# In each chunk of the projections, VectorE takes the row maxima of the fourth turn before the statistics of the next rows, and the variances directly follow the statistics

## The reference

```
def attention(x, Wq, Wk, Wv, Wo, bo):
    q, k, v = (split_heads(x @ W) for W in (Wq, Wk, Wv))
    scores = einsum('bhqd,bhkd->bhqk', q, k) * 16 ** -0.5
    scores = where(causal, scores, -inf)
    out = softmax(scores) @ v
    return merge_heads(out) @ Wo + bo

x = x + attention(layernorm(x), ...)
x = x + int8_matmul(layernorm(x), rhs)
```

## Time and profile before

| | us |
|---|---|
| runs of the kernel before | 1672.59, 1675.17, 1675.41 |
| their median | 1675.17 |
| the profiled execution, device time | 1670.0 |
| its span, first to last instruction | 1668.2 |
| TensorE busy | 1562.9 (94%) |
| VectorE busy | 1522.0 (91%) |
| ScalarE busy | 1362.6 (82%) |
| GpSimd busy | 290.9 (17%) |
| mean granted clock of TensorE | 0.981 |

### The profile page before, as it was taken

One profiled execution on the slowest core, in us unless ns is written; L12 is line 12 of the kernel. 1 busy time (PEld: TensorE's weight loads), 2 busy tenths in 40 slices (PEclk: granted clock), 3 DMA queues, 4 the chain that ended last, 5 costly groups with the idle time before them and its releaser, 6 DMA issues.

```text
span 1668.2 us, 40684 instructions
## 1 busy us (share of the span) xinstructions
PE 1562.9 (94%) x16715; PEld 623.8 (37%) x16715; DVE 1522.0 (91%) x1839; ACT 1362.6 (82%) x2659; POOL 290.9 (17%) x397
## 2 busy tenths in 40 slices
PE   4799989999999999999999999999999999999965
PEld 2444433333333333333333333333333333344433
DVE  5589889999999999999999999999999999578876
ACT  3355559999999999999999999999999999877651
POOL 5343401211111111111121111120202020100120
PEclk9899999999999999999999999999999999999986
DMA  2454320101121212111111212121212142034532
GB/s 82 141 161 144 124 65 17 51 18 51 43 63 43 63 52 55 57 50 60 47 60 47 60 47 59 47 61 52 62 51 63 48 119 78 15 116 134 154 118 70
DMA packets 105613, 118.79 MB, mean 71 GB/s; under 512 B 20688, under 2 KB 87508, under 8 KB 105428
## 3 DMA queue, kind: packets, MB, share of 16 engines
q1 hardware_dynamic: 105428, 116.19, 23.4%
HBM read 66.81 MB, written 48.76 MB: 69 GB/s over the span
## 4 chain that ended last, share of the span: by engine, by line
DVE 54%; PE 27%; DMA 1%; ACT 1%; issue 1%; SPq 1%; POOL 0%; ACTq 0%; DVEq 0%
DVE pmax L355 46%; PE psum L1155 12%; PE psum L1136 6%; DVE pblk L355 4%; PE psum L263 3%; PE psum L1196 3%; PE psum L277 2%; PE psum L282 2%; DMA f_rs<-inverse_sums 1%; DVE V L1438 1%; ACT prob L1326 1%; DVE V L1457 1%; DVE V L1445 1%; PE psum L1220 1%; DVE f_amax L1463 1%
## 5 line engine op out<-in xcount | busy, mean ns | idle before, releaser
L1326 ACT ACTIVATE prob<-psum 128x512 f32<-128x512 f32 (+1 forms) x2304 | 1180.9, 574 | 136.4 <-PE psum L1136 113.0
L355 DVE TENSOR_REDUCE pmax<-psum 128x2 f32<-128x1024 f32 (+1 forms) x960 | 1100.9, 1216 | 12.7 <-PE psum L282 6.6
L1155 PE MATMUL psum<-prob,V 128*32 128x256 f32 x8704 | 675.7, 391 | 0.0
L1136 PE MATMUL psum<-Q,K 50*128 50x512 f16 (+3 forms) x2560 | 465.1, 350 | 3.8 <-ACT prob L1326 1.0
L1392 POOL TENSOR_SCALAR_AFFINE_SELECT prob<-prob 128x512 f32<-128x512 f32 x256 | 160.6, 640 | 1177.6 <-ACT prob L1326 1175.1
L263 PE MATMUL psum<-K,Q 48*128 48x512 f16 x1536 | 298.4, 384 | 20.3 <-DVE pmax L355 19.4
L1155 PEld LDWEIGHTS psum<-prob,V 128*32 128x32 f32 x8704 | 181.4, 108 | 294.1 <-issue 213.8
L1136 PEld LDWEIGHTS psum<-Q,K 50*128 50x128 f16 x2560 | 174.7, 94 | 251.5 <-ACT prob L1326 185.1
L263 PEld LDWEIGHTS psum<-K,Q 48*128 48x128 f16 x1536 | 74.3, 93 | 265.8 <-DVE pmax L355 219.7
L355 DVE TENSOR_REDUCE pblk<-psum 128x8 f32<-128x1024 f32 x128 | 151.8, 1219 | 5.9 <-PE psum L282 5.7
L282 PE MATMUL psum<-K,Q 48*128 48x512 f16 (+3 forms) x1024 | 129.0, 299 | 0.0
(11 more groups left out here) (122 smaller groups left out, 709.4 us busy)
## 6 DMA issues: line engine op xcount, KB each, us to landing
f_x<-in_L_attn_x SPq DMA_DIRECT2D x32, 512.0 KB, 4.0
unnormalised<-ust SPq DMA_DIRECT2D x64, 256.0 KB, 2.9
q_parts<-part SPq DMA_DIRECT2D x64, 128.0 KB
k_parts<-part SPq DMA_DIRECT2D x64, 128.0 KB
Q<-q_parts SPq DMA_DIRECT2D x128, 64.0 KB, 2.5
K<-k_parts SPq DMA_DIRECT2D x128, 64.0 KB, 2.0
out<-V SPq DMA_DIRECT2D x16, 512.0 KB, 3.3
f_rs<-inverse_sums SPq DMA_DIRECT2D x28, 256.0 KB
```

Source lines behind the costliest of these rows:

```text
L355: nc.vector.tensor_reduce(to, of, axis=AX.X, op=ALU.max).then_inc(M.mx_free, 1)
L1136: m = nc.tensor.matmul(PS[:, SB + i % RING, at:at + n], K[it % 2][rows, pair, kb * P:(kb + 1) * P], Q[it % 2][rows, pair, (c + 1) * CH - n ...
L1155: m = nc.tensor.matmul(PS[32 * h:32 * h + 32, UB, to:to + n], V[:, it // NG * NT + kb, col:col + 32], prob[(it * NSTEP + k) % PRING][:, h, ...
L1326: nc.scalar.activation(prob[g % PRING][:, h, 0:n], PS[:, SB + i % RING, 0:n], ACT.Exp, scale=by).then_inc(exp_done, 1)
```

## The change

In the loop over chunks on VectorE, `turns(n, 3)` moves ahead of `statistics(n + 2)`. The statistics and the variances then stand directly behind each other, and the turn of place 4 follows them. Nothing else is changed, and no instruction is added or removed; on the other engines the order stays.

```
                 low_part(n, 2)
                 turns(n, 2)
                 low_part(n, 3)
+                turns(n, 3)
                 if n + 2 < NC:
                     statistics(n + 2)
-                turns(n, 3)
-                if n + 2 < NC:
                     variance(n + 2)
                 turns(n, 4)
                 if n + 2 < NC:
```

## The result

| | before | changed |
|---|---|---|
| median of 5 runs, us | 1673.45 | 1662.75 |
| lowest and highest, us | 1669.43, 1675.41 | 1660.10, 1675.05 |
| profiled execution, us | 1670.0 | 1660.1 |
| span, us | 1668.2 | 1658.3 |
| busy TensorE, VectorE, us | 1562.9, 1522.0 | 1563.1, 1523.2 |

The ratio is 0.995 with a 95% interval of 0.9926 to 0.9975. One of the five executions of the changed kernel stands apart, with 1675.05 us at a mean granted clock of 0.933, where the others have 0.979 to 0.982 and 1660.10 to 1665.53 us; it widens the interval. On two further occasions, with six executions of the changed kernel each, the ratio was 0.9923 (0.9908 to 0.9937) and 0.9928 (0.9912 to 0.9944). The changed kernel is faster by 0.5 to 0.8%. The forecast was a gain of 12.3 us, to 1662.9 us; the medians of the table differ by 10.7 us.

The account below looks back on a forecast made before the run. Prediction: TensorE and VectorE wait for each other once per projection chunk, and both are nearly full in attention. Gains of 6.5 + 5.8 = 12.3 us from 1675.2 gave 1662.9 us, range 1659 to 1668 us.

Parts of the forecast that it names:

- The place and the mechanism of the steady chunks: Turn of place 3 ahead of the statistics removes TensorE's wait of 0.79 us; TensorE becomes the bound at 11.3 us.
- the term of 6.5: Chunks 5 to 13: TensorE's removed waits for row maxima, together 6.5 us off.
- the term had 6.0: Chunks 6 to 13, within the 6.5 us: seven waits of 0.80 us and one of 0.42, 6.0 us off.
- Variances right behind the statistics: VectorE, each steady chunk: an exposed wait of 1.43 us makes turn 4 0.11 us later, hidden in idle time, 0.24 us left.
- Chunks 2 to 4: Early chunks with late x: the turn runs before x arrives, but SP's loads limit how much gain is passed on.
- the term of 5.8 us: Gain up to the first low part of chunk 5, from 98.24 to 92.4 us; bounds 2.2 and 6.2 us.
- The clock: TensorE behind the 4.41 us wait in chunk 2: full clock might bring 2.3 us more; not counted, kept as a rival.
- rival 2: Clock returns and loads come in time in the early chunks: 15.0 us off in all, 1660.2 us, chance 0.06.
- The gain of 2.3 us: Value and projection matmuls behind chunk 2's wait at full clock instead of about half: 2.3 us less, not counted.
- The attention stage takes nothing back: Stage after the projections stays as long as before; the rival that the gain is given back, 1673 to 1675 us, had chance 0.08.
- GpSimd's chain: Normalisation before the transposes keeps a margin near 1.8 us, costing nothing; the rival that it holds them, 1680.0 us, had chance 0.04.

Follow-up runs that it names:

- the run with chunks 2 to 4 alone: The new order in chunks 2 to 4 only, the old order from chunk 5 on, against the kernel before: one time of 1673.58 us.
- the second profile of the changed kernel: The kernel as changed, unaltered, run against the kernel before on another occasion: median 1660.35 against 1672.86 us, ratio 0.9923.
- the first profile's F: Time of the first score matmul of the attention stage in the first profile of the kernel before: 231.70 us.
- before again: The kernel before, unaltered, run once more for a second profile: 1676.76 us in its one time.
- the changed kernel's third profile: The kernel as changed, unaltered, run once more as partner of other runs: median 1661.42 us, ratio to before 0.9928.

## Why the prediction was right, step by step

*The place and the mechanism of the steady chunks: right.* TensorE's wait in front of the turn of place 5 went whole, TensorE became the bound, and the chunk took 11.27 us from the first projection to the next chunk's (114.61 to 125.88) against 11.3 forecast. From the first projection of chunk 5 to that of chunk 14 it went from 204.76 - 96.12 = 108.64 us to 193.33 - 90.93 = 102.40: 6.24 us against the term of 6.5. That the two agree is partly luck, since two differences cancel. Chunks 6 to 13 took 96.68 us before and 90.16 after, 6.5 us less where the term had 6.0: each became 0.86 us shorter and not 0.80. The idle time of 0.79 us is counted from the recorded end of the value matmuls; without a wait the next matmul starts before that end (124.23, where the value matmuls end at 122.82 + 1.49 = 124.31). Chunk 5 took 12.24 us instead of 11.96, where the term had it 0.51 shorter, since TensorE waits 0.7 us in it for a VectorE that the x of chunk 4 held. Doubling the statistics in both orders shows them on the loop in full in the old order (1.31 us a chunk); in the new one they cost 0.9 us a chunk, through VectorE's own time.

*Variances right behind the statistics: right.* 1.43 us start to start, hidden in VectorE's idle time, which went to 0.16 us where 0.24 were worked out.

*Chunks 2 to 4: mechanism right, the term of 5.8 us too large.* The load for chunk 3 was issued at 73.44 rather than 72.80 and landed in 4.07 us, so that the statistics stood at 77.51, not 76.7. The landing of the K stores, which the sum took from the row before at 2.65 us, took 3.75, and their issue 2.77 rather than 2.4. The low part of chunk 5 came at 94.48, not 92.4: 3.8 us of gain instead of 5.8 by that landmark. By TensorE's, the first projection of chunk 5, it was 96.12 - 90.93 = 5.2 us, since TensorE had run ahead of VectorE there. 5.2 + 6.2 is the 11.4 us found. Other profiles spread widely here: the first projection of chunk 5 came between 89.92 and 92.89 us in five kernels and repeats with the new order and the old loads in chunks 2 to 4, and between 94.18 and 96.58 in four with the old order. The means are 91.0 and 95.7, a gain of 4.7 us. What the forecast did not see is that this term cannot be priced by itself: the run with chunks 2 to 4 alone shows, in one profile, that it is lost again where the chunks behind still park their turn behind the x.

*The clock: neither the one nor the other.* The value matmuls behind the removed wait did run at the full rate (1.48 us in place of 2.74), as rival 2 had it. But behind the new wait of 2.18 us at the start of chunk 3 the granted clock was 0.57, and six projection matmuls took 2.74 us there. The gain of 2.3 us, which the forecast did not count, did not appear; the late load holds VectorE and, through the turns, TensorE too. The rule of the Trainium skill (TensorE: Matmul & The Clock Gate, Part 1: The HAM clock gate) is that waiting brings half the clock and sustained work releases it. The trace agrees at these two places (0.53 behind the wait of 4.41 us, 0.57 behind that of 2.18, and 1.00 from 71 to 80 us). Not every wait of about 2 us costs the clock: behind a wait of 1.77 us in the second profile of the changed kernel, and behind six of seven waits of 2.1 us in the old order with doubled statistics, the clock stayed at 1.00.

*The attention stage takes nothing back: right,* 1340.0 to 1341.6 us in all fourteen profiles. *GpSimd's chain: right,* no transposes wait for it in any steady chunk (in chunk 5 one of their weight loads waits 0.24 us); it starts 0.28 us behind the reciprocal (126.55 to 126.83) and its 2.16 us are what they were beside VectorE's turn.

The total agrees with the forecast better than its parts deserve. That 1662.9 met 1662.75 us is luck: the forecast started from a median of 1675.2 for before, which in five executions is 1673.45, and its gain was 1.6 us too large. Over the three pairs of medians and profiles, 12.3 us stood against 10.7 to 12.5 in the medians (10.7, 12.5, 12.4), while the projections gave 11.4, 10.4 and 12.3 us against the first profile's F (9.5, 8.4 and 10.3 against the second's), and the last stage adds several us of chance in each execution.

## What to carry to other kernels

When two engines wait for each other once per loop, look at what stands between the instruction that is waited for and its own inputs on an in-order engine: work that nobody needs yet belongs behind it, and a wait for a DMA even more so. Such a reordering is worth about the wait that it removes, here 0.79 us of idle time and 0.86 us of each steady chunk, and puts the next bound close behind, here 0.2 us away. Gains in a stretch that is fed by a queue with a pace of its own need not add to the gains of the others; and to judge a change of under 1%, measure the stage it is in, by a landmark in the trace and in several profiles: here the last stage varied by 7.6 us and the landmark by 1.9, where the change was worth some 11.

## What the runs showed of the hardware

The last stage of one and the same program took 96.0 us in one execution and 103.6 in another. On average TensorE's granted clock lies between its two levels, 1.2 and 2.4 GHz, there, and it falls at other points in each of the two executions: in the second 8 us behind the staging it is 1.00 in the one and 0.69 in the other. The table of stretches from the staging to a point halfway, for before, before again and the changed kernel's third profile:

```profile
1572.10:1620.10 48.00, 38.03 (x298) 20.33 (x298) 38.70 (x90) 26.88 (x61) 7.74 (x9) 0.87 0.41 124
```

```profile
1571.30:1623.10 51.80, 40.76 (x290) 20.63 (x290) 38.64 (x86) 26.31 (x60) 7.49 (x9) 0.82 0.39 114
```

```profile
1559.80:1609.30 49.50, 38.95 (x296) 20.64 (x297) 38.31 (x89) 26.91 (x60) 8.15 (x9) 0.86 0.41 122
```

VectorE does the same work in each (38.3 to 38.7 us), TensorE takes 38.0, 40.8 and 39.0 us for nearly as many matmuls at a granted clock of 0.87, 0.82 and 0.86. The order of the clocks is that of the lengths. Over the whole last stage of all fourteen profiles the granted clock is 0.76 and 0.77 in the two shortest (96.0 and 96.9 us), 0.75 or 0.76 in the ten between and 0.73 in the two longest (101.3 and 103.6 us). VectorE's busy time differs there as well, 71.3 and 74.4 us in the two profiles of before. That the clock is the cause was not tested by a run.

The time from a DMA's issue to its landing is not a constant of its size: in the changed kernel a load of x of 512 KB took 3.8 to 4.1 us (60.72 to 64.50, 73.44 to 77.51, 86.51 to 90.37), and with the loads moved right behind the stores of K 5.5 and 6.4 us. It took 5.8 us without that move too, for chunk 5 in the run with chunks 2 to 4 alone (98.15 to 103.91), with eight stores issued right behind it; the load at 86.51 has such stores behind it as well, so the cause of the 5.8 us stays open. All these times end where VectorE, waiting, starts on the x. The last stores of K in chunk 3 landed in 2.65 us in the kernel before and in 3.75 us in the changed one, where a load of x and eight stores were issued in one go. I had taken both from single rows as if they were constants.
